# Macaron layer (mixture FFN, banded attention, mixture FFN) on 8 cores: the transposed copies of z made by DMA, and the hand-over from the first FFN to attention cut into smaller steps

## The chip, the cores and the metric

One Trainium2 chip, 8 cores, each with its own half of one batch element: 16 row tiles of 128 tokens, and a 17th that attention needs as neighbour. The cores do not exchange data. The metric is the device time of the slowest core in microseconds.

## The reference, cut to what matters

```python
def ffn(x, U, V, W1, b1, W2, b2):            # K = 8 parts of rank R = 64
    h = relu(einsum('bsd,de->bse', x, W1) + b1)
    alpha = softmax(einsum('bse,ek->bsk', h, W2) + b2)
    vx = einsum('krd,bsd->bskr', V, x)
    uvx = einsum('kdr,bskr->bskd', U, vx)
    return einsum('bsk,bskd->bsd', alpha, uvx)
def attn(x):                                  # 16 heads of 128, blocks of 64,
    q, k, v = heads(x @ Wq), heads(x @ Wk), heads(x @ Wv)
    scores = q @ k.T * 128 ** -0.5 + mask     # mask: |block i - block j| <= 2
    return merge(softmax(scores) @ v) @ Wo
x = x + 0.5 * ffn(layernorm(x))
x = x + attn(layernorm(x))
x = x + 0.5 * ffn(layernorm(x))
```

D is 2048. The tensor `z` of the kernel is `alpha * vx` (512 numbers a token), and the FFN's output is `z @ U`.

## The kernel before

Each engine has a list of instructions and waits in the order in which the Python program emits them, so the written order is the order of work on every engine. SyncE (SP) issues plain DMAs and all DMA transposes (`dma_turn`, L102); GpSimd (POOL) issues the loads that cast f32 weights to bf16 (L95), and a `pow` of each layer norm (L311).

**First FFN.** The 17 tiles go in five blocks, `BLOCKS`, of 5, 3, 3, 3 and 3 tiles. A block has 16 pieces `w1` (L385): one 128-column slice `e` of W1 times up to three tiles, 16 matmuls into one PSUM bank. ScalarE (ACT) makes relu of it into one of three buffers `hT` (L392), and `logits` (L406), tiny matmuls with W2, is emitted one piece behind, after the next piece's matmuls. Between the pieces stand hooks: layer norm `ln1` of coming tiles (VectorE, DVE: four `bn_stats` L305, aggregate L307, L310, then the normalisation L323), their transposes, `ln2` of the tiles just done, loads of x, and `ln2_store` of the normalised tile `xn2` to DRAM. Then `vu` (method of `Layer`): for each tile `v` (L437, 16 matmuls of 512 columns), softmax once after the first, `z` (DVE, L448), `zturn` (four 128x128 TensorE transposes L289 into PSUM and a copy by ACT, L458, into `zT`), and `u` (L469, four banks of four matmuls of 512 columns, each added into x by DVE, L474). For three tiles the order on TensorE (PE) is v0, v1, turn0, v2, turn1, u0, turn2, u1, u2. After `u`, SP stores the tile (`x1d`).

**Seam.** Attention keeps all 17 normalised and transposed tiles in `xn2T`, which lies over W1 in SBUF (tile t over slice t). `load_xn2T` reads a group of tiles back from DRAM through DMA transposes once the slices' last use is over: in the last block group 0 at piece 4, groups 1 and 2 at piece 8, group 3 at piece 12, group 4 after piece 15, and group 5 (tiles 14 to 16) in attention. The first weight slabs of attention (`load_slab`, wk, wq, wv of pair 0: 128x4096 each) are loaded whole, when `ln2` of tiles 10, 11 and 12 has freed the x buffer below.

**Attention** runs over 8 pairs of heads and 6 groups of tiles: `proj` makes K, K, Q, Q (L721) and then V for each tile (L711), in three banks in turn (`banks3`); K and V are copied by ACT (L728, L715), Q is scaled by DVE (L733). Between the projections the `unit`s of earlier groups are laid: `scores` (L810), masking and maximum by DVE, exponentials by ACT (L824), `weights` (DVE), `turn` (a 128x768 DMA transpose, PTs<-Pn) and seven slots later `values` (L850). Before the first projection stand `ln2(14)`, `ln2(15)` and three memsets (L788) on DVE; `ln2(16)` stands after the fourth projection.

**Output** (`wo_piece`, L977) and **last FFN** (`final`, the same `Layer`) follow, the latter in six groups of 3, 3, 2, 3, 3 and 2 tiles.

## Time and profile before

| | |
|---|---|
| three runs | 1811.45, 1816.94 and 1996.73 us |
| median of them | 1816.94 us |
| the profiled execution | 1813.04 us |
| its span, slowest core (core 3) | 1811.4 us |
| spans of the 8 cores | 1794.1 to 1811.4 us |
| PE busy | 1736.0 us, 96% of the span |
| DVE, ACT, POOL busy | 43%, 24%, 11% |

The span runs from the first to the last instruction of one core; the execution's own time lies 1.6 us above it. PE is busy nearly always, so time can be lost or won in two ways: where PE stands still or runs at the lower of its clocks, and by matmuls that are no longer issued.

### The profile page before, as it was taken

The numbers are of one execution on the slowest core, as the hardware profiler recorded it, in microseconds if no ns is written. First come the engines' busy times: TensorE is split into PE (matmuls) and PEld (weight loads), VectorE is DVE, ScalarE is ACT, GpSimd is POOL, SyncE is SP. The second block draws the span as 40 slices with busy tenths as digits, with TensorE's granted clock in tenths as the row PEclk, the third lists the DMA queues.
The fourth block names the chain that finished last, engine by engine and source line by source line (L and its number), as shares of the span: only waits on it lengthen the run. The fifth ranks groups of instructions, "written<-read, shape, count | busy, mean of one in ns | idle before, by whom it ended". The sixth has DMA issues, their size and how long they took to land.

```text
span 1811.4 us, 34807 instructions; the slowest of 8 cores (1794.1 to 1811.4 us)
## 1 busy us (share of the span) xinstructions
PE 1736.0 (96%) x12724; PEld 1149.9 (63%) x12724; DVE 787.0 (43%) x1633; ACT 429.8 (24%) x1035; POOL 192.2 (11%) x318
## 2 busy tenths in 40 slices
PE   3999999989899999999999999979999999999998
PEld 3867655545577777777777777755444455576556
DVE  5047657506354555545454545434213334143421
ACT  2312311111233333333333333321000011111111
POOL 2001022000111111111111111110000000011000
PEclk9999999989999999999999999989999999999999
DMA  9946566499954545555555456999890684154211
GB/s 208 180 103 215 159 140 176 119 58 164 187 83 75 80 72 84 74 75 78 72 81 77 68 82 95 127 146 226 219 328 25 114 154 143 44 155 126 94 70 48
DMA packets 256217, 218.37 MB, mean 121 GB/s; under 512 B 194480, under 2 KB 232368, under 8 KB 244784
## 3 DMA queue, kind: packets, MB, share of 16 engines
q1 hardware_dynamic: 215056, 120.62, 31.1%
q0 software_dynamic: 38976, 89.70, 28.2%
q10 hardware_dynamic: 2016, 5.81, 1.0%
q8 instruction: 104, 1.70, 0.4%
q14 instruction: 65, 0.53, 0.1%
HBM read 168.93 MB, written 59.24 MB: 126 GB/s over the span
## 4 chain that ended last, share of the span: by engine, by line
PE 84%; SPq 7%; DMA 4%; DVE 3%; issue 1%; ACT 1%; POOL 0%; DVEq 0%; ACTq 0%; POOLq 0%
PE R L721 23%; PE R L385 17%; PE R L711 12%; PE R L977 12%; SPq L102 6%; PE R L437 5%; PE R L469 4%; PE pX L385 4%; PE R L850 2%; DVE lnb L305 2%; DMA W1a<-w 2%; DMA PTs<-Pn 1%; PE pX L437 1%; PE pX L469 1%; PE pX L810 1%; PE pS L810 1%
## 5 line engine op out<-in xcount | busy, mean ns | idle before, releaser
L711 PE MATMUL R<-wvS,xn2T 128*128 128x256 bf16 x2176 | 255.4, 275 | 3.3 <-DVE Qb L733 3.3
L721 PE MATMUL R<-xn2T,wkS 128*128 128x384 bf16 (+1 forms) x1536 | 251.5, 317 | 0.0
L721 PE MATMUL R<-xn2T,wqS 128*128 128x384 bf16 (+1 forms) x1536 | 240.5, 310 | 0.0
L711 PEld LDWEIGHTS R<-wvS,xn2T 128*128 128x128 bf16 x2176 | 214.1, 99 | 35.7 <-issue 3.9
L385 PE MATMUL R<-xnTa,W1a 128*128 128x256 bf16 (+2 forms) x1648 | 205.3, 283 | 24.2 <-issue 9.0
L977 PE MATMUL R<-Wo,Ob 128*128 128x512 bf16 x1024 | 222.6, 379 | 0.0
L721 PEld LDWEIGHTS R<-xn2T,wkS 128*128 128x128 bf16 x1536 | 150.1, 98 | 82.1 <-issue 0.6
L721 PEld LDWEIGHTS R<-xn2T,wqS 128*128 128x128 bf16 x1536 | 151.0, 99 | 75.5 <-issue 3.1
L385 PEld LDWEIGHTS R<-xnTa,W1a 128*128 128x128 bf16 x1648 | 141.6, 99 | 69.3 <-issue 25.8
L385 PE MATMUL R<-xnTc,W1c 128*128 128x384 bf16 (+1 forms) x1232 | 185.1, 307 | 0.0
L977 PEld LDWEIGHTS R<-Wo,Ob 128*128 128x128 bf16 x1024 | 99.9, 98 | 118.9
L385 PEld LDWEIGHTS R<-xnTc,W1c 128*128 128x128 bf16 x1232 | 115.1, 97 | 52.1
L305 DVE BATCH_NORM_STATS2 lnb<-Xa 128x6 f32<-128x512 f32 x136 | 94.4, 694 | 86.6 <-DMA Xa<-x 71.9
L824 ACT ACTIVATE Praw<-pX,att 128x384 f32<-128x384 f32 x128 | 74.4, 581 | 237.5 <-DVE att L821 231.5
L834 DVE TENSOR_SCALAR Pn<-Praw,att 128x384 bf16<-128x384 f32 (+1 forms) x256 | 106.6, 417 | 37.6 <-DVE att L832 23.6
L824 ACT ACTIVATE Praw<-pS,att 128x384 f32<-128x384 f32 (+1 forms) x128 | 72.7, 568 | 195.6 <-DVE att L821 189.4
L981 DVE TENSOR_TENSOR Xc<-Xc,R 128x512 f32<-128x512 f32 x64 | 44.0, 688 | 152.4 <-PE R L977 142.8
L311 POOL TENSOR_TENSOR lnb<-lnb,mhalf 128x1 f32<-128x1 f32 x50 | 51.1, 1022 | 508.2 <-DVE lnb L310 507.7
L859 DVE CAST ost<-R 128x256 bf16<-128x256 f32 x128 | 54.4, 425 | 110.7 <-PE R L850 91.6
L419 DVE TENSOR_TENSOR lgb<-pX,B2b 128x24 f32<-128x24 f32 (+2 forms) x11 | 2.0, 183 | 230.7 <-PE pX L406 230.7
L392 ACT ACTIVATE hTa<-R,b1T 128x384 bf16<-128x384 f32 (+2 forms) x103 | 50.3, 488 | 192.4 <-PE pX L406 154.2
L392 ACT ACTIVATE hTc<-R,b1T 128x384 bf16<-128x384 f32 (+1 forms) x77 | 42.0, 545 | 202.4 <-PE pX L406 132.0
(100 smaller groups left out, 1684.0 us busy)
## 6 DMA issues: line engine op xcount, KB each, us to landing
x1d<-Xa SPq DMA_DIRECT2D x16, 1024.0 KB, 4.2
y<-Xc SPq DMA_DIRECT2D x16, 1024.0 KB, 4.5
Xa<-x POOLq DMA_DIRECT2D x10, 1024.0 KB, 9.2
Xc<-x1d POOLq DMA_DIRECT2D x9, 1024.0 KB, 19.6
xn2d<-xna SPq DMA_DIRECT2D x17, 512.0 KB, 5.3
W1a<-w POOLq DMA_DIRECT2D x16, 512.0 KB, 43.4
Wo<-wo POOLq DMA_DIRECT2D x32, 256.0 KB, 5.7
x2d<-Xc SPq DMA_DIRECT2D x8, 1024.0 KB, 15.2
```

What stands on the lines that cost most here:

```text
L102: self.queue["sync"].append(("op", lambda e: e.dma_start_transpose(dst, src), sem, 16))
L305: p.op("vector", lambda e, j=j: e.bn_stats(st[:, j * 6:j * 6 + 6], x[:, j * 512:(j + 1) * 512]), token, *free)
L385: tok = p.mm(lambda en, c=c: en.matmul(bank[:, 0:w], slot[:, off + c * 128: off + (c + 1) * 128], view(self.xnT, place * D + c * 128, (D, ...
L392: relu = p.op("scalar", lambda en: en.activation(h[:, 0:w], bank[:, 0:w], AF.Relu, bias=b1T[:, e:e + 1]), tok, cst["b1t"], *free)
L437: tok = p.mm(lambda e, c=c, o=o: e.matmul(bank[:, :], self.xnT[:, o:o + 128], self.V[:, c * 512:(c + 1) * 512], start=(c == 0), stop=(c == ...
L469: done = p.mm(lambda e, kc=kc, bank=bank, cg=cg: e.matmul(bank[:, :], zT[:, kc * 128:(kc + 1) * 128], self.U[:, kc * D + cg * 512: kc * D ...
L711: tok = p.mm(lambda e, c=c, o=o: e.matmul(bank[:, 0:256], xn2T[:, o:o + 128], wvS[s][:, c * 256:(c + 1) * 256], start=(c == 0), stop=(c == ...
L721: tok = p.mm(lambda e, c=c: e.matmul(bank[:, 0:w], wS[:, c * 256 + k * 128: c * 256 + (k + 1) * 128], view(xn2T, a * D + c * 128, (D, n), ...
L824: ex = p.op("scalar", lambda e, h=h: e.activation(Praw[b][:, h * 384 + c0:(h + 1) * 384], bank[:, h * 512 + c0: h * 512 + 384], AF.Exp, bi ...
L834: kept["nm"] = p.op("vector", lambda e, h=h: e.tensor_scalar_mul(Pn[u % 3][:, h * 384 + c0:(h + 1) * 384], Praw[b][:, h * 384 + c0:(h + 1) ...
L859: O_ended[0] = p.op("vector", lambda e: e.tensor_copy(ost[o][:, (t - a) * 256:(t - a + 1) * 256], R[3][:, 0:256]), tok, ost_store[o])
L977: tok = p.mm(lambda e, h=h, o=o: e.matmul(bank[:, :], Ob[:, o:o + 128], Wo[cg][:, h * 512:(h + 1) * 512], start=(h == 0), stop=(h == 15)), ...
```

## The change

1. **z turned by transfers.** `zturn` becomes a DMA transpose of 128x512 on SP's queue, from SBUF to SBUF; there are three `zt` and four `zT` buffers. In `vu` each z is turned right after its v, and `u` follows three tiles behind. Between the last v and the first u that is left stands a `filler`: piece 0 of the next block (or group); in the last block of the first FFN the two K projections of pair 0, group 0 (`first_k`), in the five banks of the FFN. At the kernel's end there is none.
2. **Logits two pieces behind**: `logits(1)` leaves the newest finished piece for later; `vu` drains with `logits(0)` after the first v.
3. **Slabs in eighths.** The slabs of pair 0 are loaded as eighths of 128x512, one a piece: wk in pieces 8 to 15 of the fourth block, wq in 3 to 10 and wv in 8 to 15 of the last.
4. **Tiles turned one by one.** In the last block tile t of `xn2T` is loaded at piece t + 2, for t from 0 to 8, tiles 9 and 10 after the block's `vu`.
5. **The last six from chip.** Tiles 11 to 16 are not stored to DRAM but turned from the normalised tile in SBUF (`turn_xn2`): 11 to 13 after `vu`, 14 to 16 after projections 3, 5 and 6 of group 0.
6. Q of pair 0, group 0 is scaled by ACT instead of DVE; the x1 tiles 14 and 15 are stored by POOL's queue instead of SP's.

```diff
@@ class Layer
+        def logits(self, keep):
+            while len(self.late) > keep:
+                self.logits_of(*self.late.popleft())
...
         def zturn(self, z, tok):
-            bank, done = transposes(lambda j: z[:, j * 128:(j + 1) * 128], 4, [tok])
-            self.zt.give(z, done)
             zT, free = self.zT.take()
-            end = p.op("scalar", lambda e: e.copy(
-                zT[:, :], pT[:, bank * 1024: bank * 1024 + 512]), done, *free)
-            tbank["ended"][bank] = end
+            end = p.dma_turn(S(zT.name), view(zT, 0, (128, 4), (1, 128)), z[:, :], tok, *free)
+            self.zt.give(z, end)
             return zT, end
...
             for k in range(n):
                 i, tok = self.v(places[k])
                 if k == 0:
-                    self.logits()
+                    self.logits(0)
                     self.softmax(blk, n)
-                zs[k] = self.z(blk, k, i, tok)
+                z = self.z(blk, k, i, tok)
                 hook(("v", k))
-                if k >= 1:
-                    turn(k - 1)
-                if k >= 2:
-                    up(k - 2)
-            if n == 2:
-                up(0)
-            turn(n - 1)
-            for k in range(max(1, n - 2), n):
+                if k >= 3:
+                    up(k - 3)
+                zT[k] = self.zturn(*z)
+            if filler:
+                filler()
+            for k in range(max(0, n - 3), n):
                 up(k)
@@ seam
+    def turn_xn2(t, *tokens):
+        if t not in ln2_b:
+            flush_ln()
+        b, tok = ln2_b[t]
+        end = p.dma_turn(S(f"tx{place[t]}"), view(xn2T, t * D, (128, 16), (1, 128)), b[:, :],
+                         tok, *tokens)
+        xn2T_tok.setdefault(GROUP_OF[t], []).append(end)
+        norm.xn.give(b, end)
...
+    def first_k():
+        for k in range(2):
+            proj("k", 0, 0, k, banks5)
...
         if last_blk:
-            for e, gs in ((4, (0,)), (8, (1, 2)), (12, (3,))):
-                for q in gs:
-                    pairs.append((e, lambda q=q, e=e: load_xn2T(q, first.w1_done[(blk, e - 1)])))
+            pairs += [(3 + i, lambda i=i: slab_part("q", 11, i, e=3 + i)) for i in range(8)]
+            pairs += [(8 + i, lambda i=i: slab_part("v", 12, i, e=8 + i)) for i in range(8)]
+            pairs += [(t + 2, lambda t=t: load_xn2T(t, first.w1_done[(blk, t)]))
+                      for t in range(9)]
         run_items(blk, [(0, e) for e in range(16)], at_hooks(pairs))
+        vu_a(blk, {})
         if last_blk:
-            load_xn2T(4, first.w1_done[(blk, 15)])
-        vu_a(blk, {})
+            for t in (9, 10):
+                load_xn2T(t, first.w1_done[(blk, 15)])
+            for t in (11, 12, 13):
+                turn_xn2(t, first.w1_done[(blk, 15)])
```

PE at the seam before, from the last block's second v to the first V projections (xnTa: tiles of the block, wkS and wqS: slabs of attention, Qb and Kb: its Q and K):

```order
L437 MATMUL pX<-Va,xnTa 128x512 x16
L289 MATMUL pS<-idb,zta_77 128x128 x4
L437 MATMUL R<-Va,xnTa 128x512 x16
L289 MATMUL pS<-idb,zta_78 128x128 x4
L469 MATMUL R<-Ua,zTa_81 128x512 x12
L469 MATMUL pX<-Ua,zTa_81 128x512 x4
L289 MATMUL pS<-idb,zta_77 128x128 x4
L469 MATMUL R<-Ua,zTa_79 128x512 x16
L469 MATMUL pX<-Ua,zTa_80 128x512 x4
L469 MATMUL R<-Ua,zTa_80 128x512 x12
L721 MATMUL R<-xn2T,wkS_95 128x384 x32
L721 MATMUL R<-xn2T,wqS_97 128x384 x32
```

and now:

```order
L438 MATMUL pX<-Va,xnTa 128x512 x16
L438 MATMUL R<-Va,xnTa 128x512 x16
L728 MATMUL R<-xn2T,wkS_97 128x384 x32
L467 MATMUL R<-Ua,zTa_82 128x512 x4
L467 MATMUL pX<-Ua,zTa_82 128x512 x4
L467 MATMUL R<-Ua,zTa_82 128x512 x8
L467 MATMUL R<-Ua,zTa_83 128x512 x8
L467 MATMUL pX<-Ua,zTa_83 128x512 x4
L467 MATMUL R<-Ua,zTa_83 128x512 x4
L467 MATMUL R<-Ua,zTa_80 128x512 x12
L467 MATMUL pX<-Ua,zTa_80 128x512 x4
L728 MATMUL R<-xn2T,wqS_99 128x384 x32
```

The transposes of z are gone, and the two K projections of the first group have moved ahead of the three u.

SP's queue at the same place before, from the stores of block four's tiles on (xn2d: normalised tiles in DRAM):

```order
L95 DMA x1d<-Xa_66 128x2048
L95 DMA x1d<-Xa_67 128x2048
L95 DMA xn2d<-xna_71 128x2048
L102 DMA_TRANSPOSE xn2T<-xn2d 128x16x128 x3
L95 DMA xn2d<-xna_73 128x2048
L95 DMA xn2d<-xna_70 128x2048
L102 DMA_TRANSPOSE xn2T<-xn2d 128x16x128 x11
L95 DMA x1d<-Xa_61 128x2048
L95 DMA x1d<-Xa_62 128x2048
```

and now:

```order
L95 DMA x1d<-Xa_66 128x2048
L95 DMA x1d<-Xa_67 128x2048
L102 DMA_TRANSPOSE xn2T<-xn2d 128x16x128 x9
L102 DMA_TRANSPOSE zTa_82<-zta_79 128x4x128
L102 DMA_TRANSPOSE zTa_83<-zta_77 128x4x128
L102 DMA_TRANSPOSE zTa_80<-zta_78 128x4x128
L102 DMA_TRANSPOSE xn2T<-xn2d 128x16x128 x2
L102 DMA_TRANSPOSE xn2T<-xna_71 128x16x128
L102 DMA_TRANSPOSE xn2T<-xna_73 128x16x128
```

The three turns of z stand behind nine turns of `xn2T`, and the stores of tiles 11 to 16 to `xn2d` and of x1 14 and 15 have left the queue.

DVE at attention's head before (xna: normalised tiles 14 and 15, then the memsets, the two Q of group 0, and `ln2(16)`):

```order
L323 TENSOR_SCALAR xna_72<-Xa_62,lnb_142 128x2048
L788 MEMSET Pn_85 128x768
L788 MEMSET Pn_86 128x768
L788 MEMSET Pn_87 128x768
L733 TENSOR_SCALAR Qb_105<-R 128x384 x2
L305 BN_STATS lnb_141<-Xa_63 128x6 x4
```

and now:

```order
L323 TENSOR_SCALAR xna_72<-Xa_62,lnb_146 128x2048
L808 MEMSET Pn_87 128x768
L808 MEMSET Pn_88 128x768
L808 MEMSET Pn_89 128x768
L305 BN_STATS lnb_145<-Xa_63 128x6 x4
L307 BN_AGGR lnb_145<-lnb_145 128x2
L310 TENSOR_SCALAR lnb_145<-lnb_145 128x1
L323 TENSOR_SCALAR xna_71<-Xa_63,lnb_145 128x2048
L836 MEMSET pS 64x2x64
L841 TENSOR_REDUCE att_155<-pS 128x2
```

The two Q have left DVE; the layer norm of tile 16 now stands directly ahead of the first unit's maximum.

## Rows read from the trace of the kernel before

**Rows 1.** The page's part 1: busy us of each engine, share, instructions.

```profile
PE 1736.0 (96%) x12724; PEld 1149.9 (63%) x12724; DVE 787.0 (43%) x1633; ACT 429.8 (24%) x1035; POOL 192.2 (11%) x318
```

**Rows 2.** Spans and granted clock of the cores.

```profile
core 0: 1806.9 us, clock 0.991
...
core 3: 1811.4 us, clock 0.989
...
core 7: 1800.1 us, clock 0.993
```

**Rows 3.** Waits of PE over the span, core 3: total us, times, longest.

```profile
PE pX L406 <- ACT hTa L392: 4.5, 3, 1.7
...
PE R L469 <- ACT zTc L458: 3.3, 4, 0.8
```

**Rows 4.** Timeline of PE at the seam, core 3: start, us, instruction [idle before <-releaser].

```profile
388.39 1.95 PE L385 MATMUL R<-xnTa,W1a 128*128 128x384 bf16 x11
399.38 1.76 PE L385 MATMUL R<-xnTa,W1a 128*128 128x384 bf16 x5 [9.04 <-issue]
...
439.99 6.46 PE L711 MATMUL R<-wvS,xn2T 128*128 128x256 bf16 x32 [3.32 <-DVE Qb L733]
...
468.93 0.59 PE L850 MATMUL R<-PTs,Vb 128*128 128x128 bf16 x4 [5.92 <-DMA PTs<-Pn]
```

**Rows 5.** A window at the seam, core 3: engines' busy us, PEclk, DMA share, GB/s.

```profile
400.00:405.00 5.00, 5.00 (x17) 1.95 (x16) 0.00 (x0) 0.58 (x1) 0.00 (x0) 0.52 1.49 37
```

**Rows 6.** Timeline of SP at the seam, core 3.

```profile
359.41 54.56 SPq L102 DMA_TRANSPOSE xn2T<-xn2d  x3
...
415.32 39.31 SPq L102 DMA_TRANSPOSE xn2T<-xn2d  x11
```

**Rows 7.** DMA from 455 to 480 us, core 3: packets, MB, share; issues to landing.

```profile
q0 software_dynamic: 1008, 0.92, 31.2%
...
xn2T<-xn2d SPq DMA_TRANSPOSE x3, 7.6
```

**Rows 8.** Windows of core 0: seam, then end of attention.

```profile
350.00:500.00 150.00, 136.50 (x938) 87.27 (x936) 65.24 (x127) 30.46 (x73) 16.43 (x25) 0.95 0.95 142
1170.00:1230.00 60.00, 48.72 (x337) 32.93 (x335) 22.86 (x57) 15.02 (x43) 8.99 (x17) 0.89 1.05 146
```

**Rows 9.** The same windows of core 7.

```profile
350.00:500.00 150.00, 146.68 (x1031) 95.71 (x1030) 72.39 (x144) 34.27 (x84) 17.97 (x27) 0.99 0.91 151
1170.00:1230.00 60.00, 43.35 (x298) 28.43 (x297) 18.78 (x46) 11.41 (x33) 6.02 (x12) 0.89 1.03 144
```

**Rows 10.** Timeline of block four's v and u, core 3, all engines.

```profile
330.39 3.61 PE L437 MATMUL R<-Va,xnTa 128*128 128x512 bf16 x16
...
332.66 0.69 DVE L448 TENSOR_TENSOR zta<-R,alb 128x512 bf16<-128x512 f32 x1
...
337.52 0.39 PE L289 MATMUL pS<-idb,zta 128*128 128x128 bf16 x4
337.74 3.62 PE L469 MATMUL R<-Ua,zTa 128*128 128x512 bf16 x16
```

**Rows 11.** Tile PTs (128x768): its DMA transposes, issue to landing.

```profile
DMA to landing us min/median/max: 2.7/3.7/23.0
```

**Rows 12.** Tile xnTa (128x2048): its DMA transposes, issue to landing.

```profile
DMA to landing us min/median/max: 4.3/4.8/10.1
```

**Rows 13.** Timeline of DVE at attention's head, core 3.

```profile
425.42 3.08 DVE L305 BATCH_NORM_STATS2 lnb<-Xa 128x6 f32<-128x512 f32 x4
...
438.42 0.70 DVE L788 MEMSET Pn<- 128x768 bf16 x1 [0.30 <-DVE Pn L788]
...
440.68 3.09 DVE L305 BATCH_NORM_STATS2 lnb<-Xa 128x6 f32<-128x512 f32 x4
...
445.26 1.34 DVE L323 TENSOR_SCALAR xna<-Xa,lnb 128x2048 bf16<-128x2048 f32 x1 [0.87 <-POOL lnb L311]
```

**Rows 14.** The page's part 5: the exponentials.

```profile
L824 ACT ACTIVATE Praw<-pX,att 128x384 f32<-128x384 f32 x128 | 74.4, 581 | 237.5 <-DVE att L821 231.5
```

More of the change, by code:

```diff
@@ L206, in build_nc @@
     hTa = [at(f"hTa{s}", 200704 + 768 * s, 384, BF16) for s in range(3)]
-    zta = [at(f"zta{s}", 203008 + 1024 * s, 512, BF16) for s in range(2)]
-    zTa = [at(f"zTa{s}", 205056 + 1024 * s, 512, BF16) for s in range(3)]
+    zta = [at(f"zta{s}", 203008 + 1024 * s, 512, BF16) for s in range(3)]
+    zTa = [at(f"zTa{s}", 206080 + 1024 * s, 512, BF16) for s in range(4)]
     xn2T = at("xn2T", 0, NT * D, BF16)
@@ L478, in u, with vu @@
             return add
-        def vu(self, blk, places, xs, added, hooks):
+        def vu(self, blk, places, xs, added, hooks, filler=None):
             n = len(places)
-            zs, zT = {}, {}
+            zT = {}
             def hook(key):
@@ L617, in w1a, with call @@
         first.w1(blk, t - BLOCKS[blk][0][0], n, place[t], e, [xnT_tok[q] for q in range(t, t + n)])
+    def call(f, *args):
+        return lambda: f(*args)
     def vu_a(blk, hooks):
         ts = tiles_a(blk)
-        first.vu(blk, [place[t] for t in ts], [xa(t) for t in ts], added_a(blk), hooks)
+        filler = call(w1a, blk + 1, 0, 0) if blk + 1 < len(BLOCKS) else first_k
+        first.vu(blk, [place[t] for t in ts], [xa(t) for t in ts], added_a(blk), hooks, filler)
     def at_hooks(pairs):
@@ L688, in build_nc, with load_xn2T @@
     xn2T_tok = {}
-    def load_xn2T(g, *tokens):
-        for t in range(GROUPS[g][0], sum(GROUPS[g])):
-            xn2T_tok[g] = p.dma_turn(S(f"lxn{g}"), view(xn2T, t * D, (128, 16), (1, 128)),
-                                     rows(xn2d, t), xn2_tok[t], *tokens)
+    def load_xn2T(t, *tokens):
+        xn2T_tok[GROUP_OF[t]] = [p.dma_turn(
+            S(f"lxn{GROUP_OF[t]}"), view(xn2T, t * D, (128, 16), (1, 128)), rows(xn2d, t),
+            xn2_tok[t], *tokens)]
+    def turn_xn2(t, *tokens):
[6 more added lines that the diff above has]
+        norm.xn.give(b, end)
     kq_end = {}
@@ L704, in proj @@
         w = n * 128
-        i, bank, ended = banks3.next()
-        p.wait("tensor", slab_tok[(kind, pr)], xn2T_tok[g], ended)
+        i, bank, ended = banks.next()
+        p.wait("tensor", slab_tok[(kind, pr)], *xn2T_tok[g], ended)
         if kind == "v":
@@ L746, in free_then, with slab_part @@
         def free_then(t):
-            def then():
-                if t + 7 < NT:
-                    load_x(t + 7, "gpsimd")
-                elif t % 7 in (3, 4, 5):
-                    load_slab({3: "k", 4: "q", 5: "v"}[t % 7], 0, None, *x_last[t])
-            ln2(t, then)
+            ln2(t, call(load_x, t + 7, "gpsimd") if t + 7 < NT else None)
+        def slab_part(name, t, part, blk=blk, e=0):
+            load_slab(name, 0, part, *x_last[t], first.w1_done[(blk, e - 1)])
         pairs = []
@@ L1107, in build_nc @@
         assert not hooks, hooks
[L1108 removed]
+        final.vu(i, [place_c[t] for t in ts], [Xc[slot_c[t]] for t in ts], done_c(g), {},
+                 call(w1c, i + 1, 0) if i + 1 < NG else None)
     p.wait("sync", *y_tok)
```

66 lines of the change are left out of this document (34 added, 32 removed).

## The prediction

> **What bounds the kernel now.** I read the page's busy times first: PE is busy 96% of the span [rows 1]. Matmuls back to back run at their size: 16 of 512 columns take 16 x 512 / 2.4 GHz = 3.4 us, 16 of 384 columns 2.6 us, 16 of 256 1.7 us, and I call those a v or a u, a three-tile piece, and a V projection. DVE, ACT and POOL are far from full, so this change can pay only where PE stands still, where it runs at 1.2 GHz, or where a matmul goes.
>
> Then PE's waits and its timeline. At the seam of core 3 stand three long gaps: 9.04, 3.32 and 5.92 us [rows 4], and the window of the whole seam gives 150 - 131.0 = 19.0 us of idle on this core; on core 0 the same window has 150 - 136.5 = 13.5 [rows 8] and on core 7 only 3.3 [rows 9]. Behind each gap PE goes on at the lower clock: after the first the granted clock is 0.52 in five busy us, a loss of 2.4 [rows 5]; after the second 32 matmuls of 256 columns take 6.46 us instead of 3.5 [rows 4]; with a smaller loss after the third I put core 3 at 7 us of slow clock. So the seam costs core 3 26 us, core 0 about 17 (13.5 and an estimated 4), core 7 about 5 (3.3 and 1.8).
>
> The first gap is named "issue": it lies in the middle of a piece, waits for no operand, and comes while three turns hold SP's queue for 54.56 us; the next eleven take 39.31 us, 3.6 each [rows 6]. In those 54 us two whole slabs were under way. The third is the first unit's turned weights, late behind the queue. The second is common to all cores: DVE works off two layer norms and three memsets before it empties Q's bank.
>
> What matters for the sum: the metric is the slowest core, and the cores lose their time in different places. Core 3 is slowest at 1811.4 only by its seam; core 7 has 1800.1 [rows 2] with nearly none, and loses 60 - 43.35 = 16.7 us at the end of attention where core 0 loses 11.3 [rows 8, 9], a place that the change does not touch. The gain of core 3 therefore can't be the gain of the kernel.
>
> **The change part by part.**
>
> *z's transposes leave PE.* Four transposes take 0.22 us, from 337.52 to the u at 337.74 [rows 10]. There are 17 + 16 = 33 z: 33 x 0.22 = -7.3 us, all of it on PE's path, on every core. ACT loses 33 copies, which cost nothing and give nothing.
>
> *Are the turned z in time?* In block four v0 ends about 330.3, and softmax and z end at 332.66 + 0.69 = 333.35, so z0 exists 3.0 us after v0's end [rows 10]. No row shows a 128x512 turn. The nearest are 128x768, landing after 2.7 to 3.7 us (23.0 at worst) [rows 11], and 128x2048 after 4.3 to 4.8 (10.1 at worst) [rows 12]; I take 3.5, with 2.7 and 23 as ends. The first u of a three-tile block comes after v1, v2 and the filler: 3.5 + 3.5 + 2.6 = 9.6 us after v0. The turned z is there after 3.0 + 0.1 + 3.5 = 6.6. Margin 3.0; z1 and z2 have more. Cost nothing in ten of the eleven passes, as long as a turn lands within 6.5 us.
>
> The Trainium skill (VectorE: DVE Perf Modes, "The three transpose paths" and "Rules for kernel authors") gives 390 ns for a 128x128 transpose on TensorE, 1309 ns by DMA, and advises TensorE wherever PSUM will do. Four by DMA would then be 5.2 us: in time for three-tile blocks, late by some 2 us in each of the two passes of two tiles, and the sum would be 4 us higher. The 128x768 turns of this trace, six such squares in 3.7 us, speak against that figure.
>
> *Passes of two tiles.* Before, each u there waits 0.82 us for ACT's copy, four times, 3.3 us in all [rows 3]. In the middle one the filler (three tiles, 2.6 us) now covers v0's end to 3.5 + 2.6 = 6.1 against 5.8 to 6.8 for the turned z: -1.5. At the kernel's end there is no filler: u0 starts at 5.8 to 6.8 instead of 3.5 + 0.22 + 0.82 (and a few tenths), about 4.7; u1 then follows without its own 1.1 of turn and copy. Between -0.1 and +0.9 net, of which the transposes are already counted: +0.8.
>
> *The filler in block two* wants tile 10, whose turn is queued on SP behind that of the first z. z0 3.1 us, the issue 1.2, the landing 4.6: 8.9 us after v0, but the filler could start at 7.1: +1.8. In the long first block the tiles 5 and 6 have four more v or u of cover, nothing; z3 and z4 stand there behind a store of x1 and have a u, a v and the filler over, 0 to 2, I take 0.
>
> *Logits.* Three waits for relu sum to 4.5 us, the longest 1.7 [rows 3]; ACT is then in a long normalisation. One piece more is 1.8 us of slack for two-tile pieces (the 1.09 wait goes) and 0.9 for one-tile pieces (two waits of 1.7 fall to 0.8): -2.9.
>
> *The transfers of the seam.* Nine turns at 3.6 us need 32 us, with the slab eighths beside them perhaps 4 each, 36. They can start when the last x1 store is queued, 1.5 us into the last block, and the first z turn is due 15 pieces and a v later, at 46 us. So they are through, and neither K (filler) nor u has to wait. That eighths and turns go together the stretch from 455 shows: 0.92 MB of eighths beside turns that land in 7.6 us [rows 7]. Gaps one and three and what follows them go on all cores. The bounds: nothing of it goes if the collision is the turns' own (26 us stay on core 3), all of it goes otherwise.
>
> *What is late next.* DVE. At attention's head it needs 439.12 - 425.42 = 13.7 us for layer norms 14 and 15 and the memsets, then 446.60 - 440.68 = 5.9 for 16 [rows 13]. Call E the end of the last u. DVE starts at E + 1.1 and is free at E + 20.8. PE used to reach the first scores late, with K, K and a wait of 3.3 behind it. Now both K lie before E and Q is emptied by ACT, so PE goes on: Q, Q, V, V, V, K, scores 0 at E + 12.2, K, Q, scores 1, Q, and stands at E + 18.1 before the V projection that reuses the bank of the second K. ACT must copy that bank, but ahead of the copy stand the first unit's two exponentials, and they wait for DVE's maximum, E + 21.8. Two exponentials with their accumulator reads and the copy: 581 ns each at full width [rows 14], 1.8 us in all. PE goes on at E + 23.6: a new wait of 5.5 us and, as after the 3.3 us one, about 2 us at the lower clock. +7.5 on every core. The first unit's turn is issued near E + 25 and wanted after E + 33, so that is hidden.
>
> **The sum.** Common: -7.3 - 1.5 + 0.8 + 1.8 - 2.9 = -9.1. Per core, old seam out, new one in: core 3: 1811.4 - 26 + 7.5 - 9.1 = 1783.8. Core 0: 1806.9 - 17.5 + 7.5 - 9.1 = 1787.8. Core 7: 1800.1 - 5.1 + 7.5 - 9.1 = 1793.4. Core 7 is now the slowest. Its 16.7 us at attention's end against 11.3 of core 0 may fall to another core or be less next time, so the slowest core is between 1788 and 1794; I take 1791.5, and with the 1.6 us that the profiled execution lies above its span, 1793. That is 20 us under this execution (1.1%), 24 under the median shown.
>
> **The rivals.**
>
> *Seam wholly hidden.* If DVE's norms do not hold PE (the new 7.5 us are 0 to 2), and no core has core 7's luck at attention's end, the slowest is core 0 or its like at 1780, so 1779 to 1782. For it: the gap is a chain of four estimates. Against: the order leaves no other work for PE there. Chance 0.16, part of it over 2%.
>
> *Little net.* The seam's gain is only core 3's, and the contention at attention's end grows, since all cores now arrive there together: core 7 had the least seam and the largest loss there. Two more waits of 5 us or a seam wait of 12 instead of 5.5 give 1803 to 1806. Chance 0.16.
>
> *The turned z come late, slower than before.* z is the only path to u, and it now shares SP's queue and the DMA rings with stores, loads and cast weights. A turn on this chip has taken 10.1 us beside a whole slab [rows 12] and 23.0 in attention's last stretch [rows 11]. If 10.1 were usual, each pass would wait 3.6 us and lose about 2 at the lower clock: 11 x 5.6 = 62, 1793 + 62 = 1855. It decides from a landing of 6.5 us on; break-even with before is at 20 us, 1.8 a pass. Against it: in every pass of before the big stores and loads start after the u, not between v and u, and the medians are 3.7 and 4.8. Chance 0.04.
>
> **How the numbers follow.** Forecast 0.64, seam hidden 0.16, little net 0.16, late z 0.04. The range takes in the first three with the bounds of the last estimates (turn 2.7 to 5, new seam wait 0 to 12, attention's end 11 to 17): 1777 to 1808. Faster by over 2%, about what a measurement of this kernel can tell from no change, needs less than 1780.6 from the median 1816.9: most of the first rival and a tail of the forecast, 0.14. Slower by over 2%: 0.03. The rest, 0.83, is within 2%.
>
> **What would show it right or wrong.** Right: no transposes of zta in PE's groups; the turns of zTa land under 5 us and no wait of L467 (the u's line now) above 1 us outside the two-tile passes; SP's nine turns near 4 us each and no "issue" gap in W1; PE waits at the first V of group 1 for ACT's copy of K, with an exponential ahead of it, some 5 us after some 18 from the last u; cores 3 and 7 change places. Wrong: waits of u for DMA zT in several passes (late z); turns of xn2T still over 10 us beside the eighths (the collision is not of size); a head of attention without a wait (DVE estimate wrong); or end-of-attention waits well over 17 us on some core.

## The result, and the profile after

The changed kernel takes 1799.4 us (median of 17 executions), the kernel before 1812.3 (median of 17 beside them): a ratio of 0.9939, 95% interval 0.9925 to 0.9952, so 0.6% faster, where 1.1% was forecast (1793 us). The time lies inside the range given. In some executions of either kernel four or all eight cores had a lower granted clock and took longer; such executions are in the medians, but not in the ratios, nor in the means over cores and the spreads given below. The profiled execution took 1803.9 us; its cores:

```profile
core 0: 1799.2 us, clock 0.990
core 1: 1801.6 us, clock 0.990
core 2: 1791.4 us, clock 0.991
core 3: 1781.3 us, clock 0.994
...
core 7: 1780.2 us, clock 0.993
```

Against [rows 2], core 3 went from 1811.4 (slowest) to 1781.3 and core 7 from 1800.1 to 1780.2, and core 1 now has 1801.6. But this is one execution: over 15 of them the slowest core is 1, 0, 2, 0, 5, 3, 6, 2, 6, 0, 4, 4, 7, 7, 6, and core 7 alone lies anywhere from 1778.9 to 1802.7. The eight cores of one execution lie 17.6 us apart on average, and their mean is 1788.2. The page's busy times, against [rows 1]:

```profile
PE 1731.7 (96%) x12592; PEld 1144.2 (64%) x12592; DVE 785.9 (44%) x1631; ACT 410.9 (23%) x1004; POOL 205.0 (11%) x341
```

There are 132 fewer matmuls: 33 z of four transposes. PE's waits on core 3, against [rows 3]:

```profile
PE R L718 <- ACT Kb L735: 6.2, 1, 6.2
PE pS L289 <- DVE xnc L323: 3.2, 2, 2.5
PE pS L289 <- ACT xna L333: 3.0, 1, 3.0
PE R L467 <- DMA zTc<-ztc: 2.3, 2, 2.1
PE R L870 <- DMA PTs<-Pn: 2.1, 1, 2.1
PE R L385 <- DMA xnTa<-xna: 1.9, 1, 1.9
PE pX L407 <- ACT hTa L392: 1.9, 2, 1.2
```

The waits for `relu` fell from 4.5 to 1.9 us, and the gap of 9.04 us in W1 [rows 4] is gone. Three waits are new: one of 6.2 us at the seam, one of 3.0 us in block two for a layer norm whose normalisation ACT does (L333), one of 1.9 us for tile 10. The waits of u for a turned z are in the two-tile passes alone, 2.3 us in all, where ACT's copy of z cost 3.3. The seam on PE, core 3:

```profile
403.47 5.36 PE L728 MATMUL R<-xn2T,wkS 128*128 128x384 bf16 x32
408.67 1.03 PE L467 MATMUL R<-Ua,zTa 128*128 128x512 bf16 x4
...
419.03 5.36 PE L728 MATMUL R<-xn2T,wqS 128*128 128x384 bf16 x32
...
431.44 1.91 PE L728 MATMUL R<-xn2T,wkS 128*128 128x256 bf16 x16
...
435.25 1.91 PE L728 MATMUL R<-xn2T,wqS 128*128 128x256 bf16 x16
443.32 5.73 PE L718 MATMUL R<-wvS,xn2T 128*128 128x256 bf16 x32 [6.16 <-ACT Kb L735]
```

The last u ends at 419.03; the wait of 6.16 us comes 18 us later, and the 32 matmuls behind it take 5.73 instead of 3.65 us: 2.1 us lost at a lower clock (granted clock 0.62 from 443 to 449 us). It is 6.15 or 6.16 us on all eight cores. Why ACT is late, from ACT's and DVE's timelines of core 3:

```profile
431.47 0.37 ACT L735 CAST Kb<-R 128x256 bf16<-128x256 f32 x1 [1.37 <-PE R L728]
441.44 0.47 ACT L844 ACTIVATE Praw<-pS,att 128x256 f32<-128x256 f32 x1 [9.60 <-DVE att L841]
...
442.81 0.37 ACT L735 CAST Kb<-R 128x256 bf16<-128x256 f32 x1
```

```profile
420.43 3.09 DVE L305 BATCH_NORM_STATS2 lnb<-Xa 128x6 f32<-128x512 f32 x4
...
431.44 0.70 DVE L808 MEMSET Pn<- 128x768 bf16 x1 [0.29 <-DVE xna L323]
...
434.23 3.09 DVE L305 BATCH_NORM_STATS2 lnb<-Xa 128x6 f32<-128x512 f32 x4
...
440.66 0.69 DVE L841 TENSOR_REDUCE att<-pS 128x2 f32<-128x512 f32 x1
```

The second K of group 1 is finished on PE at 433.35 (431.44 + 1.91), but ACT's copy of it, at 442.81, stands behind two exponentials that wait for DVE's maximum at 440.66, and that stands behind three layer norms and three memsets. SP's queue there, against [rows 6]:

```profile
354.41 50.79 SPq L102 DMA_TRANSPOSE xn2T<-xn2d  x9
405.30 3.74 SPq L102 DMA_TRANSPOSE zTa<-zta  x3
```

Nine turns hold the queue for 50.8 us, 5.6 each, not 4 (44.3 to 50.8 us on the eight cores). The turns of z on this core, issue to landing, first those of the first FFN (tile zTa), then those of the last (zTc):

```profile
DMA to landing us min/median/max: 2.4/2.4/4.6
```

```profile
DMA to landing us min/median/max: 2.4/2.4/3.2
```

And the two windows of rows 8 and 9, on core 0, then core 7:

```profile
350.00:500.00 150.00, 143.84 (x979) 91.76 (x976) 72.26 (x139) 30.48 (x75) 26.02 (x41) 0.98 0.89 140
1170.00:1230.00 60.00, 47.09 (x335) 31.41 (x334) 21.51 (x53) 13.99 (x40) 7.50 (x15) 0.91 1.05 153
```

```profile
350.00:500.00 150.00, 143.84 (x1003) 93.58 (x1002) 71.47 (x141) 32.40 (x81) 27.02 (x43) 0.98 0.82 134
1170.00:1230.00 60.00, 57.53 (x377) 35.19 (x376) 29.48 (x70) 14.42 (x41) 6.33 (x12) 0.97 1.09 233
```

At the seam both cores now stand idle for the same 6.2 us (150 - 143.84). At the end of attention core 7 stood still for 16.7 us before and for 2.5 here; core 0 for 12.9 (11.3 before).

What went from the seam was above all the gap that core 3 has third in [rows 4]. Cores 0 to 5 of the kernel before each waited 5.1 to 9.4 us for the first unit's turned weights (PTs), cores 6 and 7 not at all; the gap named "issue" stood on two cores only, 9.0 us on core 3 and 1.9 on core 1. Core 0 before:

```profile
459.31 0.59 PE L850 MATMUL R<-PTs,Vb 128*128 128x128 bf16 x4 [9.20 <-DMA PTs<-Pn]
```

Neither gap is there on any core of the changed kernel.

To place gains, PE's timeline of each core is cut at marks: the start of a block's last u matmul, the first V projection of attention's group 2, the first and the last Wo matmul, the end. Us, median of the eight cores, lowest and highest in brackets for the seam and end:

| kernel | to end of block 1 | block 2 | blocks 3, 4 | block 5 and seam | attention | output | last FFN | end |
|---|---|---|---|---|---|---|---|---|
| before | 149.2 | 70.6 | 128.4 | 114.7 (107.8-128.9) | 754.3 | 232.4 | 352.5 | 1800.3 (1794.1-1811.4) |
| changed | 150.7 | 75.2 | 127.1 | 107.6 (107.3-108.4) | 745.0 | 235.1 | 349.0 | 1788.6 (1780.2-1801.6) |

The filler shifts work across marks: in the changed kernel block 2 holds 0.9 us more work than before (its own first piece has gone, block 3's has come), the seam 2.6 us less. So the seam gained 4.5 us on the median core (114.7 - 107.6 - 2.6) and 18 on the worst (128.9 - 108.4 - 2.6), the last FFN 3.5; block 2 lost 3.7 (75.2 - 70.6 - 0.9).

The largest change of the table is one that the sum had no term for: attention and output together are 6.6 us shorter on the median core (9.3 less 2.7). About 1.3 of it lies at attention's head. The rest lies in the last pair, where PE's waits up to the first Wo matmul were 2.4 to 15.2 us before (median core 10.2) and 0.3 to 10.8 here (5.4). Nothing of the change stands there, and these are two executions. On another chip the mean over cores and executions was 1791.9 us for the kernel before and 1787.2 and 1786.5 for two kernels close to the changed one ("Tiles turned in groups again" and "Logits one piece behind", below). That is a gain of about 5 us, near what the other stages give (12.4 less 6.6). So most of attention's 6.6 us is probably the luck of the two profiled executions.

### The profile page after: what moved, and what is told of

Same layout as the page of the kernel before. It is cut to its first block, busy times and chain, and to the rows that moved or that the text cites. A ratio compares the mean times of both kernels' runs of the same rounds, so it can differ in the third digit from the quotient of the medians.

```text
span 1801.6 us, 34591 instructions; the slowest of 8 cores (1780.2 to 1801.6 us)
## 1 busy us (share of the span) xinstructions
PE 1731.7 (96%) x12592; PEld 1144.2 (64%) x12592; DVE 785.9 (44%) x1631; ACT 410.9 (23%) x1004; POOL 205.0 (11%) x341
## 4 chain that ended last, share of the span: by engine, by line
PE 85%; DVE 6%; DMA 5%; issue 2%; ACT 1%; DVEq 0%; POOL 0%; SPq 0%; ACTq 0%; POOLq 0%
PE R L728 23%; PE R L385 19%; PE R L718 12%; PE R L996 10%; PE pX L385 5%; PE R L438 5%; PE R L467 5%; DMA PTs<-Pn 2%; PE R L870 2%; DVE lnb L305 2%; DMA W1a<-w 2%; PE pX L467 1%; PE pX L830 1%; PE pX L438 1%; PE pS L830 1%
## 5 line engine op out<-in xcount | busy, mean ns | idle before, releaser
L854 DVE TENSOR_SCALAR Pn<-Praw,att 128x384 bf16<-128x384 f32 (+1 forms) x256 | 106.6, 416 | 37.8 <-DVE att L852 23.4
L392 ACT ACTIVATE hTa<-R,b1T 128x256 bf16<-128x256 f32 (+2 forms) x102 | 49.6, 486 | 221.0 <-PE pX L407 132.1
L852 DVE RECIPROCAL att<-att 128x2 f32<-128x2 f32 x128 | 21.3, 166 | 152.2 <-ACT Praw L844 149.1
```

The costliest lines, as they stand in the source:

```text
L392: relu = p.op("scalar", lambda en: en.activation(h[:, 0:w], bank[:, 0:w], AF.Relu, bias=b1T[:, e:e + 1]), tok, cst["b1t"], *free)
L854: kept["nm"] = p.op("vector", lambda e, h=h: e.tensor_scalar_mul(Pn[u % 3][:, h * 384 + c0:(h + 1) * 384], Praw[b][:, h * 384 + c0:(h + 1) ...
```

## The experiments

Each is an edit of the changed kernel unless said otherwise. The rows of the table go on at the end.

**No filler in the first block.** The first piece of block two stands behind the last u again.

```diff
+        if blk == 0:
+            filler = None
...
-            if i > 0 or blk == 0:
+            if i > 0 or blk <= 1:
```

> Only the filler of the long first block is taken out: piece 0 of block two stands behind the last u again. Theory (the filler takes one piece of 1.8 us of cover from everything that starts with the last u: x loads, norms of tile 7, so PE now waits for ACT's xna of tile 7): that wait falls from 3.7 us on core 1 (1.5 to 4.4 on the cores) by about 1.8, what is left is logits waits under 1, the first 230 us are 2 to 4 us shorter, total -2 to -4 us. Rival (the wait comes from the loads of x themselves or from the relus two pieces late): the wait of L289 stays above 3 us and nothing changes. u must not wait for z: turns landed in 2.5 to 4.7 us.

Measured: 1802.4 us, ratio 0.9939 (0.9907 to 0.9972). In the profiled execution cores 0, 1, 4 and 5 had a granted clock of 0.83 to 0.85 over the first 230 us, and their waits can't be set beside the others'. Cores 2, 3, 6 and 7 had one of 0.97 to 0.99, so that theirs can. PE on core 2:

```profile
176.07 1.05 PE L289 MATMUL pS<-idb,xna 128*128 128x128 bf16 x16 [2.37 <-ACT xna L333]
```

On the four cores the wait for ACT's norm is 0.7 to 2.4 us (mean 1.6) against 1.5 to 4.4 with the filler (mean 3.0), close to the 1.8 less that the theory wanted. But the waits for `relu` grow from 2.3 to 3.1 on the mean, and the end of block two, which has the same work ahead of it in both kernels, comes at 224.1 to 226.7 us against 224.0 to 228.7: some 1 us earlier and not 2 to 4.

**Tile 10 turned before z.**

```diff
-    vu_a(1, at_hooks([(("v", 1), call(ln1_turn, 10))]))
+    vu_a(1, at_hooks([(("v", 0), call(ln1_turn, 10))]))
```

> Tile 10's turn is queued after the first v instead of the second, so ahead of the first turn of z. Theory: the wait of 1.9 us before the filler of block two's pass goes, with up to 1.4 us of lower clock on some cores: -2 to -3 us in the first 230 us; the first z's turn is 2 us later and still in time. Rival: the turn then waits for the norm by ACT and the wait only moves: no change.

Measured: the 1.9 us wait is gone on all cores, and block two falls from 75.2 to 73.0 us (72.2 to 73.4 on the cores, 74.8 to 77.4 in the changed kernel); 1795.8 us, ratio 0.9933 (0.9909 to 0.9957). The queue order cost block two 2.2 us; that they reach the kernel's time the interval does not show.

**Memsets on POOL.**

```diff
-        p.op("vector", lambda e, b=b: e.memset(Pn[b][:, :], 0.0))
+        pn_free[b] = p.op("gpsimd", lambda e, b=b: e.memset(Pn[b][:, :], 0.0), x_add[16])
```

> The three memsets of Pn at attention's head go from DVE to POOL. Theory (the new wait of 6.15 us at the seam is DVE's chain of norms and memsets ahead of the first maximum, with K's copy on ACT behind the exponentials): DVE reaches the maximum 3.0 us earlier, so the wait falls to 3.1 us on all cores and the run by 3 to 4 us. Rival (the wait is set by the V or K copies on ACT or by a transfer): it stays at 6.1 us.

PE at the first V of group 1, core 1:

```profile
439.50 5.14 PE L718 MATMUL R<-wvS,xn2T 128*128 128x256 bf16 x32 [3.62 <-ACT Kb L735]
```

6.15 became 3.62 (3.1 was expected), block 5 and seam 107.6 became 104.7 (-2.9); 1797.8 us, ratio 0.9911 (0.9848 to 0.9973). Three memsets, some 3 us of DVE, taken away shorten the wait by 2.5 us on every core: DVE's chain sets it.

**Q of group 0 scaled by DVE again.**

```diff
-                if (pr, g) == (0, 0):
+                if False:
```

> Undoes one edit: the Q of pair 0, group 0 is scaled by DVE again. Theory: PE then waits for Q's bank behind two norms and three memsets: it reaches that V projection at E + 7 to 9 and the bank is free at E + 14 to 15.5: a first wait of 6 to 7 us for DVE's Q, and in its place the later wait for ACT's K copy shrinks to 1 us or less, since DVE reaches the first maximum only 1.2 us later while PE is 6 us later. Total 0 to +2 us. Rival (both waits add up): +6 us or more.

```profile
433.84 6.21 PE L718 MATMUL R<-wvS,xn2T 128*128 128x256 bf16 x32 [8.86 <-DVE Qb L744]
```

This wait, for DVE's Q at an earlier V projection, comes in place of the one for ACT's copy of K, of which nothing is left (8.86 us where 6 to 7 was expected). The stretch grows by 3.3 us to 110.9, the time is 1803.6, ratio 0.9958 (0.9919 to 0.9998).

**z on TensorE again.** Transposes, ACT's copy and the order of `vu` of before, no fillers, both K back at attention's head.

```diff
         def zturn(self, z, tok):
+            bank, done = transposes(lambda j: z[:, j * 128:(j + 1) * 128], 4, [tok])
+            self.zt.give(z, done)
             zT, free = self.zT.take()
-            end = p.dma_turn(S(zT.name), view(zT, 0, (128, 4), (1, 128)), z[:, :], tok, *free)
-            self.zt.give(z, end)
+            end = p.op("scalar", lambda e: e.copy(
+                zT[:, :], pT[:, bank * 1024: bank * 1024 + 512]), done, *free)
+            tbank["ended"][bank] = end
...
-                if (kind, pr, g) != ("k", 0, 0):
-                    proj(kind, pr, g, k)
+                proj(kind, pr, g, k)
```

> Undoes part 1 alone: z is turned by TensorE and copied by ACT in the old order of v, turn and u, and there is no filler (both K stand in attention again). Theory: the two blocks of 3 tiles at 64.2 us again instead of 63.6, block two's pass 3 to 4 us shorter (the fillers' cost goes), the tail 2 us shorter, the two-tile pass 1.6 us longer; at attention's head PE has the two K back behind E, so DVE is less late: the wait for ACT's K copy falls from 6.15 to about 1 us. Sum: +7.3 + 1.5 - 4 - 2 - 7 = -4 to 0 us against the changed kernel, so part 1 gives nothing here. Rival (part 1 is what makes the kernel faster): +7 us or more.

PE at the seam, core 3:

```profile
411.75 5.36 PE L734 MATMUL R<-xn2T,wkS 128*128 128x384 bf16 x32
416.95 5.36 PE L734 MATMUL R<-xn2T,wqS 128*128 128x384 bf16 x32
...
435.70 3.65 PE L724 MATMUL R<-wvS,xn2T 128*128 128x256 bf16 x32 [0.62 <-ACT Kb L741]
```

1793.7 us, ratio 0.9941 (0.9917 to 0.9965). That ratio is the changed kernel's; but on the same chip two kernels that differ little from the changed one ("Tiles turned in groups again" and "Logits one piece behind", below) took 1800.1 and 1797.4 us, and the mean over all cores is 1782.3 against their 1787.2 and 1786.5. So undoing part 1 does not cost 7.3 us; by these figures it gains some 4, though the ratios' intervals overlap. Here the last u ends at 411.75 and the V starts at 435.70, 23.95 us later; in the changed kernel it is 443.32 - 419.03 = 24.3. So this V comes 24 us behind the last u whether the two K (5.2 us) stand between or not: the chain of DVE that starts with the last u sets it in both. The K fill the time if they stand behind the u, and are added if they stand ahead.

**Slabs whole again.** wq at piece 3, wv at piece 8, wk at piece 8 of the block before, each as one load.

```diff
-            pairs += [(3 + i, lambda i=i: slab_part("q", 11, i, e=3 + i)) for i in range(8)]
-            pairs += [(8 + i, lambda i=i: slab_part("v", 12, i, e=8 + i)) for i in range(8)]
+            pairs += [(3, lambda: slab_part("q", 11, None, e=3))]
+            pairs += [(8, lambda: slab_part("v", 12, None, e=8))]
```

> Undoes the eighths: wk, wq and wv of pair 0 are loaded whole, each at the first piece of its eighths; the tiles still come one by one. Theory (whole slabs are what starves the turns): turns of xn2T in the last block take over 20 us to land again, PE waits for turned tiles or z by the end of the block, 5 to 20 us on some cores. Rival (it was the groups of tiles that blocked SP): turns land within 10 us and the run stays as it is.

SP, then PE, of core 1:

```profile
353.38 68.12 SPq L102 DMA_TRANSPOSE xn2T<-xn2d  x9
421.60 3.74 SPq L102 DMA_TRANSPOSE zTa<-zta  x3
```

```profile
424.98 1.87 PE L467 MATMUL R<-Ua,zTa 128*128 128x512 bf16 x4 [17.18 <-DMA zTa<-zta]
```

Nine turns take 68.1 us, and since z now stands behind them in the same queue, u waits 17.18 us. That is one core of eight: on the other seven the nine took 38.9 to 51.0 us, no longer than beside eighths (44.3 to 50.8), and no u waited. Two runs, 1806.1 and 1823.4 us (the second with cores 4 to 7 at a granted clock of 0.97), too few for a ratio. In the twelve profiles with eighths the nine never took more than 53.8 us. So the eighths may take away a bad case; they don't make the average shorter, and one core of one execution is thin ground. The waits for PTs at attention's head, which six cores had before, do not come back here, nor in the next kernel. What took them away is then probably part 5 (tiles 11 to 16 from SBUF), or the x1 stores moved in part 6; no kernel undoes either by itself.

**Tiles turned in groups again** (pieces 4, 8, 8, 12), slabs in eighths.

```diff
-            pairs += [(t + 2, lambda t=t: load_xn2T(t, first.w1_done[(blk, t)]))
+            pairs += [({0: 4, 1: 8, 2: 8, 3: 12}[GROUP_OF[t]],
+                       lambda t=t: load_xn2T(t, first.w1_done[(blk, {0: 3, 1: 7, 2: 7, 3: 11}[GROUP_OF[t]])]))
```

> Undoes the tiles one by one: tiles 0 to 8 are loaded at pieces 4, 8, 8 and 12 in groups as before, the slabs stay in eighths. Theory (the eighths are enough): turns land in 5 to 10 us, the first z of the last block may be queued behind tile 8, no wait over 2 us, run unchanged. Rival (the groups pile up on SP): the turned z of the last block land late and u waits 3 us or more.

```profile
412.41 1.68 PE L467 MATMUL R<-Ua,zTa 128*128 128x512 bf16 x4 [4.88 <-DMA zTa<-zta]
```

That is core 3; on the eight cores u waits 0.4 to 4.9 us, and the median stretch grows from 107.6 to 113.0 us. The time is 1800.1 us, ratio 0.9967 (0.995 to 0.9984). By the ratio the kernel is 0.3% slower than the changed one (0.9939), which is the 5 us; by the times, taken on two chips, it is not. How much of the 5 us reaches the slowest core stays open.

**Logits one piece behind.**

```diff
-            self.logits(1)
+            self.logits(0)
```

> Undoes the logits two pieces behind. Theory: in block two the waits for relu come back, one of about 1 us ahead of tile 7's transposes (taking over part of the present wait there) and two of 1.7 to 2.6 us at the one-tile pieces instead of 0.64 to 2.1: the first 230 us are 1 to 2 us longer, everything else the same. Rival (the depth gives nothing, ACT's backlog is only met one piece later): no difference within 0.5 us.

Waits of 3.07 and 1.58 us for `relu` on core 1 take the place of 3.72 (for the norm, L333) and 0.64. The end of block two is at 226.2 us on the median core against 225.7, block two itself takes 76.3 against 75.2; 1797.4 us, ratio 0.9951 (0.9931 to 0.9971). Two behind is worth some 1 us: the PE that does not wait for `relu` waits for the norm. Cores 6 and 7 of this kernel also wait 2.5 and 2.6 us for z in the last u pass of the first FFN.

**No fillers in the first FFN, z by transfers.**

```diff
-        filler = call(w1a, blk + 1, 0, 0) if blk + 1 < len(BLOCKS) else first_k
-        first.vu(blk, [place[t] for t in ts], [xa(t) for t in ts], added_a(blk), hooks, filler)
+        first.vu(blk, [place[t] for t in ts], [xa(t) for t in ts], added_a(blk), hooks)
...
-                if (kind, pr, g) != ("k", 0, 0):
-                    proj(kind, pr, g, k)
+                proj(kind, pr, g, k)
```

> The changed kernel with z still turned by transfers, but without fillers in the first FFN; the two K projections of pair 0, group 0 are back at the head of attention. The last FFN keeps its fillers. Theory (the fillers, not the turns, gave the gain back): the wait of the norm chain in block two and the 6.15 us wait behind ACT's K copy are gone (under 1.5 us each), the last u waits under 1.5 us for its z turn in a pass, and the mark of the first V of group 2, 460.5 us in the changed kernel (median over cores) and 449.7 with z on TensorE, comes to 445 to 449; the kernel's median is 3 to 7 us below the 1793.7 of z on TensorE, if the end of attention loses the same. Rival (z by transfer is too late without cover, or the turns themselves cost elsewhere): u waits 2 us or more for the turn in each pass, and the mark is at 452 or above; the time is 1793 or more.

Block two falls from 75.2 to 70.9 us (68.9 with z on TensorE), the seam's wait to 1.0, and no u waits for z in blocks 1 to 4. In block five three cores wait; core 5, PE and SP:

```profile
407.67 4.03 PE L467 MATMUL R<-Ua,zTa 128*128 128x512 bf16 x12 [5.22 <-DMA zTa<-zta]
```

```profile
388.53 15.48 SPq L102 DMA_TRANSPOSE xn2T<-xn2d  x3
404.10 3.74 SPq L102 DMA_TRANSPOSE zTa<-zta  x3
```

The z turn lands in 2.6 us, but is issued late, behind the turns of `xn2T`; the waits are 1.2, 3.6 and 5.2 us on cores 3, 7 and 5. The mark is at 453.2 us, on the rival's side (452 or above). The median is 1794.2, ratio 0.9905 (0.9871 to 0.9939), with runs from 1783.9 on: not 3 to 7 us below 1793.7, though the mean over the cores is (1777.7 against 1782.3). So the fillers gave most of the gain back, and what one of them hid is the queue, in block five alone. Of the 2.0 us that block two still lacks against z on TensorE, 1.2 are a longer wait for ACT's norm (1.3 us against 0.1 on the mean of the cores); they come with the transfers and their order of v and u.

**TensorE turns in the first FFN, transfers and fillers in the last.** `vu_pe` and `zturn_pe` are the functions of before.

```diff
-        filler = call(w1a, blk + 1, 0, 0) if blk + 1 < len(BLOCKS) else first_k
-        first.vu(blk, [place[t] for t in ts], [xa(t) for t in ts], added_a(blk), hooks, filler)
+        first.vu_pe(blk, [place[t] for t in ts], [xa(t) for t in ts], added_a(blk), hooks)
```

> z turned by TensorE in the order of before in the first FFN, with K at the head of attention; z turned by transfers with fillers in the last FFN only. Theory (the last FFN's gain of 3.5 us stands on its own): first V of group 2 at 449.7 as with z on TensorE everywhere, last FFN 342.9 instead of 346.4 us, time 3 to 4 us below the 1793.7 of that kernel, so 1790. Rival (the gain of the last FFN is lost in its tail, 2.08 us of wait, or to the layer norms): time within 1.5 us of 1793.7.

1790.3 us, ratio 0.9900 (0.9877 to 0.9924), and the last FFN takes 348.9 instead of 352.9 us: as expected, 3.5 below the 1793.7 (measured on another chip; the intervals of the two ratios overlap, those of the stage, 347.2 to 349.1 and 352.5 to 353.5 us on the cores, do not).

**The first x1 tile loaded early**, on top of that.

```diff
+            if pr == PAIRS - 1 and g == 0:
+                load_x1(0, "gpsimd", proj_done[(PAIRS - 2, NG - 1)])
...
-                plan(slot[0] + 18, call(load_x1, 0, "gpsimd", proj_done[(PAIRS - 2, NG - 1)]))
```

> The kernel with TensorE turns in the first FFN and transfers in the last, with one more edit: the 1 MB load of the first x1 tile is issued in the last pair behind group 0's units instead of in the middle of the loads of O tiles and Wo eighths. Theory (this load is what makes the turns of PTs late there): the total wait for PTs between 1170 and 1200 us falls from 14 to 19 us on the worst cores to under 9, and the time is 6 to 10 us below that of the same kernel without the edit. Rival (the software queue is behind anyway, Wo eighths and O tiles fill it): the waits stay at 12 us or more on some core and the time within 3 us.

Between 1170 and 1205 us the longest total is 7.5 us, as the theory had it, but core 4 waits 15.2 us in all over attention's last stretch, 7.5 in that window, 4.2 at 1125 and 3.6 at 1221. 1792.5 us, ratio 0.9906 (0.9875 to 0.9937): no gain. The theory was right on the window and wrong on the time. The longest turn of PTs fell from 24.6 to 19.2 us (one execution each), so the load may have its part in the collision, but it is not the collision's only cause.

**And the O tiles behind the Wo eighths**, on top of both.

```diff
-                    plan(slot[0] + 9 + 3 * t, call(early_o, t))
+                    plan(slot[0] + 15 + 2 * t, call(early_o, t))
```

> The kernel with TensorE turns in the first FFN, transfers in the last and the x1 tile loaded early, with one more edit: in the last pair the three 512 KB loads of O tiles 0 to 2 stand behind the sixteen Wo eighths of groups 2 and 3 instead of between them. Theory (O tiles beside Wo eighths are what makes the turns of PTs wait, 13 to 19 us to land in place of 3): PTs waits of TensorE in the last pair are under 4 us on every core, the first Wo matmul comes at 1188 to 1192 us on the median core (1191 to 1196 in the two kernels before this one), the cores come within 8 us of each other, and the time is 1779 to 1785. Rival (the Wo eighths alone fill the queue, or the collision only moves to group 4, where the O tiles now stand): some core still waits 8 us or more for PTs, and the time stays at 1788 to 1793.

Tile PTs from 1130 to 1240 us, its turns' landing: the changed kernel's core 1, then this kernel's core 0.

```profile
DMA to landing us min/median/max: 2.7/8.1/23.8
```

```profile
DMA to landing us min/median/max: 2.8/6.2/16.0
```

1783.4 us, ratio 0.9845 (0.9806 to 0.9884): the fastest kernel here, 16 us under the changed one; in the profiled execution its cores lie between 1770.4 and 1781.5. The time is the one that the theory had (1779 to 1785), its path is not: the waits for PTs did not fall under 4 us (2.0 to 9.0 us a core, 2.1 to 15.1 in the changed kernel), and the first Wo matmul comes at 1194.5 us, not at 1188 to 1192. What went is the worst: four cores of the changed kernel had turns of 21 to 24 us, now the longest takes 16. Over its five comparable executions the cores lie 10.1 us apart (17.6 in the changed kernel, 15.9 and 16.1 in the last two). The median core is no faster than two kernels earlier, as the table shows:

| kernel | to end of block 1 | block 2 | blocks 3, 4 | block 5 and seam | attention | output | last FFN | end |
|---|---|---|---|---|---|---|---|---|
| z on TensorE | 148.8 | 68.9 | 128.4 | 103.6 (103.6-103.7) | 745.0 | 232.4 | 352.9 | 1780.6 (1772.3-1790.7) |
| no fillers, first FFN | 149.8 | 70.9 | 127.1 | 104.4 (103.4-110.0) | 739.1 | 233.9 | 349.0 | 1778.0 (1772.1-1789.6) |
| TensorE first, transfers last | 149.7 | 68.8 | 128.4 | 103.6 (103.6-103.6) | 738.5 | 235.5 | 348.9 | 1776.4 (1771.1-1788.3) |
| and x1 tile early | 150.3 | 70.1 | 128.4 | 103.6 (103.6-103.7) | 743.9 | 235.2 | 348.9 | 1781.7 (1774.8-1791.6) |
| and O tiles behind | 149.2 | 69.8 | 128.4 | 103.6 (103.6-103.6) | 742.8 | 235.5 | 348.9 | 1777.6 (1770.4-1781.5) |

## Why the prediction was right, and where its sizes were off

**The balance.** Direction and range held; the gain is somewhat over half the forecast (0.6% of 1.1%). 1793 was predicted and 1799.4 measured, so 6.4 us are missing. The one term that is off by that much is block two, by 5.5 us on the median core. That the rest comes out so close is in part luck: the slowest core was reckoned by a step that does not hold, and the median core's 11.7 us hold the 6.6 of attention and output, for which the sum had no term.

**The slowest core.** The sum gave each core its own losses from one execution (core 3's 26 us at the seam, core 7's 16.7 at attention's end) and so found core 7 the slowest. That step does not hold: before and after, nearly every execution has another slowest core. A reading that fits is that each core draws its loss at two places. The seam's draw, 107.8 to 128.9 us, is gone (within 1.1 us now); the draw at attention's end stays (737.8 to 752.4 us for attention on the eight cores), and sets the time. The value taken for the slowest core, 1791.5, so rests on one execution's draw.

**z's transposes leave PE.** 0.22 each was right: blocks 3 and 4 fall by 1.3 us for six z, and 16 z are in the last FFN's 3.5. But -7.3 as a gain of the whole kernel was wrong. With TensorE turns in the first FFN and K behind the u ("TensorE turns in the first FFN, transfers and fillers in the last") the ratio is 0.9900 against 0.9939, and the mark at attention's group 2 comes at 450.6 us against 460.5. What the transfers brought with them, the fillers and the K ahead of the u, cost more than 17 x 0.22 = 3.7.

**Are the turned z in time?** Yes: 2.4 us to land, below the 2.7 that was taken as the low end, and no wait of u in a three-tile pass. The late-z rival, and the estimate of 5.2 us from the Trainium skill's figure for one 128x128 square (VectorE: DVE Perf Modes, "The three transpose paths"), are refuted for turns that are issued at once; no run turns a single square by DMA, so the figure itself is not tested. The rival's mechanism is real where SP's queue is full: u waited up to 17.2 us with whole slabs, 4.9 with tiles in groups, 5.2 without the filler. In the changed kernel it was near: at the seam the first turned z landed only 0.9 us (core 3) to 5.8 us (core 7) ahead of its u, and in two kernels that differ from it elsewhere, tile 10 first and logits one behind, two cores each waited 1.0 to 2.6 us.

**Block two.** The terms were -0.7 (z), +1.8 (tile 10's turn) and -2.9 (logits), together -1.8; measured +3.7. Tile 10's wait was right (1.9, and 2.2 with it removed). Wrong was the logits term: a wait that is removed on PE is not a gain if the next wait is for something that doesn't start earlier. ACT's norm (L333) was 0 to 1.8 us late in the four kernels with TensorE turns, 0.2 to 2.3 by transfers without fillers, 1.5 to 4.4 with them, and 0.7 to 2.4 on the four comparable cores with the first block's filler alone taken out. So the filler takes cover which the norm of tile 7 had behind the last u, about 1.4 us of it. Taking it out gave little back all the same, since PE then waited for `relu`: the same mistake as in the logits term.

**The transfers of the seam.** The nine turns did not make a u wait on any core, and the first and third gap are gone everywhere, as forecast (before, the first had stood on two cores and the third on six). The size of the turns was off: 5.6 us a turn on core 3 instead of 4, the longest 23.4 us from issue to landing while the eighths of q and v went together. 36 us were reckoned for the nine and 46 were there; they took 50.8, and only the filler still covered z. That the eighths are what made the gaps go is not shown: with whole slabs, too, there was no "issue" gap on any core and no wait for PTs at attention's head.

**What is late next.** The new wait was 5.5 us and about 2 of slow clock by forecast, 6.15 and 2.1 by the trace; its place, releaser and cause are those named. With DVE's memsets taken away it is 2.5 us shorter; with Q given back to DVE, a wait of 8.86 us for that Q stands in its place. What the prediction failed to ask is what follows from it: if DVE's chain fixes the V at last u plus 24 us, the K ahead of the u buy nothing. (That V starts 23.8 to 24.2 us after the last u matmul's end on every core of the changed kernel and of all kernels that leave DVE's work there as it is, whichever side the K stand.) With them back behind it, the wait fell from 6.16 to 0.62 us and the matmuls behind it from 5.73 to 3.65: 7.6 of the 8.2 us.

**Tail and middle.** At the very end u waits 2.1 us by the trace, 2.3 to 3.3 by forecast (5.8 to 6.8 less 3.5); the last FFN gave -3.5 of -4.2.

**Little net** (1803 to 1806, by more contention at attention's end) holds in part: the slowest core is decided there. In the profiled execution PE's waits for PTs from 1000 us on are 10.1 to 15.1 us on cores 0, 1, 2 and 6 and 2.1 to 6.1 on the others; but before they were 3.1 to 17.2, so they did not grow. **Seam hidden** is refuted for this order, and came true in the kernels with K behind the u, where the seam takes 103.6 us on every core, though not with the time that went with it (1790.3 us in the kernel with transfers last, not 1779 to 1782).

## What to carry to other kernels

Work that fills a wait has to stand where the wait is: moved ahead of the event that starts the late chain, it is added to the path in full. So ask of every instruction that is moved forward what the chain after it is tied to. And where the metric is the slowest core, look over several executions for the place at which the cores differ by chance: four loads moved there, with no change in work, brought the ratio from 0.9900 to 0.9845 (1790.3 to 1783.4 us), about as much as the whole change had given. The median core did not get faster by it, the intervals of the two ratios overlap a little (0.9877 to 0.9884), and the two were measured on different chips, so the size of this gain is less sure than its direction.
